# An audio tower with expert-choice routing on one core: experts' rows re-tiled, and the threshold search split anew between VectorE and ScalarE

## The reference

```python
xf = x.reshape(bs, H)                      # 11872 x 128, layer-normed
Sm = jax.nn.softmax(xf @ W_router + b_router, axis=-1)      # 32 experts
G_ek, idx_ek = jax.lax.top_k(Sm.T, k)      # k = 11872 // 32 = 371 tokens for each expert
tokens = xf[idx_ek]
up = einsum(tokens of the group's 4 experts, W_up) + b_up   # 128 -> 341
Eout = silu(up) @ W_down + b_down                           # 341 -> 128
y = zeros.at[idx_ek].add(G_ek * Eout)      # scatter-add, and then h + y
```

## Time and profile before

| | us |
|---|---|
| median of 3 runs | 1569.08 |
| lowest, highest | 1546.99, 1583.76 |
| the profiled execution | 1576.75 |
| its span | 1575.0 |
| phase one | 0 to 1023.4 |
| threshold search | 1023.4 to 1128.6 |
| expert phase | 1128.6 to 1575.0 |

### The profile page before, as it was taken

One profiled execution on the slowest core, in us unless ns is written; L12 is line 12 of the kernel. 1 busy time (PEld: TensorE's weight loads), 2 busy tenths in 40 slices (PEclk: granted clock), 3 DMA queues, 4 the chain that ended last, 5 costly groups with the idle time before them and its releaser, 6 DMA issues.

```text
span 1575.0 us, 23738 instructions
## 1 busy us (share of the span) xinstructions
PE 1123.0 (71%) x7213; PEld 907.3 (58%) x7213; DVE 956.8 (61%) x2599; ACT 447.3 (28%) x968; POOL 604.4 (38%) x406
## 2 busy tenths in 40 slices
PE   5789879888878879879879888500267566667762
PEld 4667667677766767667657667400155455545551
DVE  2566797787787777796787777588723223232220
ACT  2132342342343232341332431433222112121210
POOL 4131221221221221221231230100168888878885
PEclk8677889879879778888788876655568667776766
DMA  2000100101001000100100100000134333333322
GB/s 71 1 16 7 33 27 19 33 28 35 14 30 32 13 26 18 32 27 13 35 26 15 35 10 17 29 12 0 29 59 69 53 62 69 54 61 59 67 42 22
DMA packets 113765, 51.13 MB, mean 32 GB/s; under 512 B 55360, under 2 KB 109920, under 8 KB 113696
## 3 DMA queue, kind: packets, MB, share of 16 engines
q1 hardware_dynamic: 49696, 36.23, 7.9%
q0 software_dynamic: 64000, 14.18, 7.2%
HBM read 30.14 MB, written 19.76 MB: 32 GB/s over the span
## 4 chain that ended last, share of the span: by engine, by line
PE 41%; issue 22%; DVE 16%; POOL 12%; DMA 6%; ACT 2%; DVEq 1%; POOLq 0%; SPq 0%; ACTq 0%
PE pa L773 6%; POOL out_dram L582 6%; PE ps L828 6%; PE pa L798 4%; POOL qd L572 4%; PE po L867 4%; PE pc L889 3%; DVE eqk L1121 3%; DMA out_dram<-tqk,idx 3%; DMA qd<-token_rows,idx 3%; PE pa L775 2%; PE pst L844 2%; PE pa L814 2%; PE po L857 1%; PE pst L842 1%
## 5 line engine op out<-in xcount | busy, mean ns | idle before, releaser
L518 POOL TENSOR_TENSOR rs<-ve,expo 106x7 f32<-106x7 f32 x48 | 71.1, 1482 | 598.2 <-DVE ve L1029 598.2
L582 POOL DMA_INDIRECT out_dram<-tqk,idx x96 | 219.2, 2283 | 46.6 <-issue 30.2
L572 POOL DMA_INDIRECT qd<-token_rows,idx x96 | 131.2, 1367 | 95.5 <-issue 86.4
L773 PE MATMUL pa<-wc,xT 128*106 128x128 f32 x896 | 135.3, 299 | 6.2 <-DMA wc<-in_L_tok_kernel_dram 6.2
L955 PE MATMUL po<-qb 114*124 114x128 f32 (+1 forms) x576 | 133.8, 400 | 1.8 <-ACT qb L730 1.8
L828 PE MATMUL ps<-qb,kd 128*106 128x212 f32 x448 | 132.7, 427 | 0.8 <-ACT kt L681 0.8
L773 PEld LDWEIGHTS pa<-wc,xT 128*106 128x106 f32 x896 | 116.9, 188 | 19.4 <-issue 8.5
L939 PE MATMUL pa<-ident,qd 124*128 124x124 f32 (+1 forms) x96 | 26.4, 408 | 134.3 <-DMA qd<-token_rows,idx 134.3
L955 PEld LDWEIGHTS po<-qb 114*124 114x124 f32 (+1 forms) x576 | 118.7, 298 | 2.8 <-issue 1.4
L529 POOL TENSOR_TENSOR qb<-qd,head_scale 64x1484 f32<-64x1484 f32 x32 | 91.9, 2873 | 67.9 <-DVE qd L1114 46.5
L867 PEld LDWEIGHTS po<-vm,P 106*53 106x53 f32 x1792 | 116.7, 141 | 0.5
(11 more groups left out here) (229 smaller groups left out, 2543.7 us busy)
## 6 DMA issues: line engine op xcount, KB each, us to landing
token_rows<-row SPq DMA_DIRECT2D x16, 463.8 KB
xT<-in_x_cols_dram SPq DMA_DIRECT2D x17, 374.5 KB, 4.4
out_dram<-h SPq DMA_DIRECT2D x16, 371.0 KB
kd<-in_L_ffn_W_up_dram SPq DMA_DIRECT2D x32, 170.5 KB
xr<-in_x_rows_dram SPq DMA_DIRECT2D x17, 224.0 KB, 10.3
qb<-in_L_ffn_W_down_dram SPq DMA_DIRECT2D x32, 114.0 KB
qb<-in_L_ffn_W_down_dram SPq DMA_DIRECT2D x32, 56.5 KB
qd<-token_rows,idx POOLq DMA_INDIRECT x96
```

The costliest lines, as they stand in the source:

```text
L518: eng.tensor_tensor(rs[:, :], ve[:, :], expo[0:C, 0, :], ALU.pow).then_inc(S[root_done], 1)
L572: eng.indirect_dma_start(out=xg[0:n, e.par, t, :], out_offset=None, in_=rows[:, :], in_offset=bass.IndirectOffsetOnAxis(ap=idx[0:n, e.k, t ...
L582: eng.indirect_dma_start(out=out_rows, out_offset=bass.IndirectOffsetOnAxis(ap=idx[0:n, e.k, t:t + 1], axis=0), in_=yw[0:n, e.par, t, :], ...
L773: eng.matmul(dst, xT[:, b.par, a:a + C], wc[:, t, :], start=(t == 0), stop=False)
```

## The change

Three things are changed together.

The experts' 371 rows lie in tiles that start at slots 0, 128 and 254. The scatters take 128, 126 and 117 rows of them. The gathers take 128, 128 and 117 rows: the second one fetches two rows that also stand at the start of the third tile, and they are not used. The slot numbers run to 382 instead of 372, and a few of their results are not used either.

In every round of the search VectorE counts 1,424 keys instead of 2,000, and ScalarE 1,544 instead of 968. ScalarE's unused output goes to the space of `tqk` instead of `xT`, which is too small for it.

The count between the two searches is done like one more round: VectorE counts 1,424 keys, ScalarE 1,544, and the goal of the second search is corrected for ScalarE's way to count.

```diff
--- before.py
+++ after.py
@@ -26,9 +26,11 @@
     F = w_up.shape[2]
     CAP = N // NE
     FC = 114
-    SL = 124
+    SL = 128
+    SLOT0, GOT, PUT = (0, 128, 254), (128, 128, 117), (128, 126, 117)
+    SLOTS = SLOT0[2] + SL
     ROW = D + NE
-    DVE_KEYS = 2000
+    DVE_KEYS = 1424
     SEG = 128 // NE
     JS = NJ // SEG
     ACT_HALF = SEG * (JS * C - DVE_KEYS) / 2
@@ -37,7 +39,7 @@
     QH = LO // 2
     LAM = 1.0 / (1.0 + 1e-07)
     EPS_W, EPS_LN, EPS_DEN = 1e-07, 1e-05, 1e-05
-    assert GS == 4 and 2 * HC == C and NC * C == LO and HALO >= C + TAPS - 1 and CAP * NE == N and 3 * FC == F + 1
+    assert GS == 4 and 2 * HC == C and NC * C == LO and HALO >= C + TAPS - 1 and CAP * NE == N and 3 * FC == F + 1 and sum(PUT) == CAP
 
     ctx = ExitStack()
     with ctx:
@@ -141,7 +143,7 @@
 
         seg_probs = qb[:, 0].rearrange("p k a b -> p (k a b)")
         seg_hits = qb[:, 1, 0].rearrange("p a b -> p (a b)").bitcast(bf16)
-        signs = xT[:, 1, :].bitcast(bf16)[:, 0:JS * C - DVE_KEYS]
+        signs = tqk[:, :, :].rearrange("p a b -> p (a b)").bitcast(bf16)[:, 0:JS * C - DVE_KEYS]
         halves = seg_probs.bitcast(u16).rearrange("p (n two) -> p n two", two=2)
         high = qb[:, 1, 1].rearrange("p a b -> p (a b)").bitcast(u16)
         low = kd[:, 0].rearrange("p a b -> p (a b)").bitcast(u16)
@@ -150,7 +152,7 @@
         same_expert = sb("same_expert", [128, 128], f16)
         bit = sb("bit", [128, 2])
         cand = sb("cand", [128, 1])
-        hits = sb("hits", [128, 2], f16)
+        hits = sb("hits", [128, 1], f16)
         sign_sum = sb("sign_sum", [128, 1], f16)
         half_expert = sb("half_expert", [128, 128], f16)
         target = sb("target", [128, 2])
@@ -164,15 +166,15 @@
         above = sb("above", [C, C], bf16)
         upto = sb("upto", [C, C], bf16)
         before = sb("before", [NJ, NJ], bf16)
-        slots_h = sb("slots_h", [NJ, CAP + 1], f16)
-        slots_f = sb("slots_f", [C, CAP + 1])
+        slots_h = sb("slots_h", [NJ, SLOTS], f16)
+        slots_f = sb("slots_f", [C, SLOTS])
         mask = sb("mask", [C, 1 + 2 * NJ], bf16)
         cnt = sb("cnt", [NJ, 2], bf16)
         cex = sb("cex", [NJ, 2])
 
-        reach = hnT[0:NJ, :].bitcast(bf16)[:, 0:2 * (CAP + 1)].rearrange("p (h n) -> p h n", h=2)
+        reach = hnT[0:NJ, :].bitcast(bf16)[:, 0:2 * SLOTS].rearrange("p (h n) -> p h n", h=2)
         dcum = sb("dcum", [NJ, 2, C], bf16)
-        inside = sb("inside", [C, CAP + 1], bf16)
+        inside = sb("inside", [C, SLOTS], bf16)
         wrap = sb("wrap", [SL, 3])
         idx = sb("idx", [SL, 4, 3], i32)
 
@@ -504,9 +506,9 @@
                                        pattern=[[1, C]], channel_multiplier=-1))
                 step(eng.affine_select(out=before[:, :], in_=before[:, :], compare_op=ALU.is_gt, fill=0.0, base=0,
                                        pattern=[[1, NJ]], channel_multiplier=-1))
-                step(eng.iota(slots_h[:, :], pattern=[[1, CAP + 1]], base=0, channel_multiplier=0,
+                step(eng.iota(slots_h[:, :], pattern=[[1, SLOTS]], base=0, channel_multiplier=0,
                               allow_small_or_imprecise_dtypes=True))
-                step(eng.iota(slots_f[:, :], pattern=[[1, CAP + 1]], base=0, channel_multiplier=0,
+                step(eng.iota(slots_f[:, :], pattern=[[1, SLOTS]], base=0, channel_multiplier=0,
                               allow_small_or_imprecise_dtypes=True))
                 assert made[0] == N_CONSTS
 
@@ -559,16 +561,13 @@
                 eng.wait_ge(row_out[p], 16 * NB // 2)
             out_rows = out.rearrange("b t d -> (b t) d")
 
-            def rows_of(t):
-                return SL if t < 2 else CAP - 2 * SL
-
             def part2(stage, what, e):
                 if (stage, what) == ("I", "idx"):
                     hold(eng, "idx_done", e.count(1, 1))
                     hold(eng, "xgt_ps", e.count(1, 1, back=2))
                     hold(eng, "gcol_done", e.count(2, 2, back=2))
                     for t in range(3):
-                        n = rows_of(t)
+                        n = GOT[t]
                         eng.indirect_dma_start(
                             out=xg[0:n, e.par, t, :], out_offset=None, in_=rows[:, :],
                             in_offset=bass.IndirectOffsetOnAxis(ap=idx[0:n, e.k, t:t + 1], axis=0)
@@ -578,7 +577,7 @@
 
                     hold(eng, y_out, e.count(48, 0))
                     for t in range(3):
-                        n = rows_of(t)
+                        n = PUT[t]
                         eng.indirect_dma_start(
                             out=out_rows, out_offset=bass.IndirectOffsetOnAxis(ap=idx[0:n, e.k, t:t + 1], axis=0),
                             in_=yw[0:n, e.par, t, :], in_offset=None, compute_op=ALU.add).then_inc(y_out, 16)
@@ -712,8 +711,11 @@
 
             eng.wait_ge(S["keys_done"], 2)
             count_signs(high, HIGH_BITS, 0, 0)
+            hold(eng, "thr_step", 2)
+            eng.activation(signs, high[:, DVE_KEYS:], ACT.Sign, scale=-1.0, bias=thr_high[:, 1:2],
+                           accum_out=sign_sum[:, :]).then_inc(S["signs_done"], 1)
             eng.wait_ge(S["keys_done"], 3)
-            count_signs(low_tied, LOW_BITS, 2 + 3 * HIGH_BITS, HIGH_BITS)
+            count_signs(low_tied, LOW_BITS, 2 + 3 * HIGH_BITS, HIGH_BITS + 1)
             eng.wait_ge(S["bup_in"], 16 * 3 * NG)
             eng.wait_ge(S["ones_done"], 1)
 
@@ -908,25 +910,19 @@
             run(eng, part)
             turn(GROUPS - 1)
 
-            def sum_hits(value, signs_value):
-
-
+            def sum_hits(value):
                 need(eng, "hits_done", value)
                 eng.matmul(pst[:, 0:1], same_expert[:, :], hits[:, 0:1], start=True, stop=False)
-                if signs_value is None:
-                    mm = eng.matmul(pst[:, 0:1], same_expert[:, :], hits[:, 1:2], start=False, stop=True)
-                else:
-                    need(eng, "signs_done", signs_value)
-                    mm = eng.matmul(pst[:, 0:1], half_expert[:, :], sign_sum[:, :], start=False, stop=True)
-                mm.then_inc(S["hits_ps"], 1)
+                need(eng, "signs_done", value)
+                eng.matmul(pst[:, 0:1], half_expert[:, :], sign_sum[:, :], start=False, stop=True).then_inc(S["hits_ps"], 1)
 
             with eng.Fori(0, HIGH_BITS // 2) as r:
                 for k in range(2):
-                    sum_hits(r * 2 + (k + 1), r * 2 + (k + 1))
-            sum_hits(HIGH_BITS + 2, None)
+                    sum_hits(r * 2 + (k + 1))
+            sum_hits(HIGH_BITS + 1)
             with eng.Fori(0, LOW_BITS // 2) as r:
                 for k in range(2):
-                    sum_hits(r * 2 + (HIGH_BITS + 2 + k + 1), r * 2 + (HIGH_BITS + k + 1))
+                    sum_hits(r * 2 + (HIGH_BITS + 1 + k + 1))
             eng.wait_ge(S["thr_step"], 8)
             eng.transpose(pst[0:C, 0:NE], thr_wide[:, :], ident[0:NE, 0:NE]).then_inc(S["thr_ps"], 1)
 
@@ -935,8 +931,8 @@
                     need(eng, x_got[e.par], e.half() * 48)
                     need(eng, "xgt_sb", e.count(1, 1, back=1))
                     for t in range(3):
-                        n = SL if t < 2 else CAP - 2 * SL
-                        mm = eng.transpose(p_xg[:, t * SL:t * SL + n], xg[0:n, e.par, t, 0:D], ident[0:n, 0:n])
+                        n = PUT[t]
+                        mm = eng.transpose(p_xg[:, SLOT0[t]:SLOT0[t] + n], xg[0:n, e.par, t, 0:D], ident[0:n, 0:n])
                     mm.then_inc(S["xgt_ps"], 1)
                 if stage == "F" and what in UP:
                     need(eng, w_in[e.k], e.m * 64 + 64)
@@ -950,9 +946,9 @@
                     need(eng, "yw_done", e.count(2, 2, back=1))
                     need(eng, "act_done", e.count(3, 3))
                     for t in [DOWN.index(what)]:
-                        n = SL if t < 2 else CAP - 2 * SL
+                        n = GOT[t]
                         for k in range(3):
-                            mm = eng.matmul(p_dn[0:n, t * D:(t + 1) * D], act[:, e.par, k, t * SL:t * SL + n],
+                            mm = eng.matmul(p_dn[0:n, t * D:(t + 1) * D], act[:, e.par, k, SLOT0[t]:SLOT0[t] + n],
                                             wdn[:, e.k, k, :], start=(k == 0), stop=(k == 2))
                     if what == DOWN[-1]:
                         mm.then_inc(S["dn_ps"], 1)
@@ -985,12 +981,12 @@
                     need(eng, "dcum_sb", e.count(1, 1))
                     need(eng, "inside_done", e.count(1, 1, back=1))
                     for h in range(2):
-                        mm = eng.matmul(p_cum[0:C, 0:CAP + 1], dcum[:, h, :], reach[:, h, :], start=(h == 0), stop=(h == 1))
+                        mm = eng.matmul(p_cum[0:C, 0:SLOTS], dcum[:, h, :], reach[:, h, :], start=(h == 0), stop=(h == 1))
                     mm.then_inc(S["cum_ps"], 1)
                 if (stage, what) == ("I", "idx"):
                     need(eng, "inside_done", e.count(1, 1))
```

(15 more changed lines are left out.)

## The result

The changed kernel takes 1453.36 us (median of 4 runs, 1439.7 to 1465.69) against 1565.26 us before (median of 4, 1546.99 to 1583.76): ratio 0.929, 95% interval 0.916 to 0.943. I had forecast 1475 with a range from 1455 to 1550: the direction and the mechanism held, the gain of 112 us was larger than the 94 of the sum, and the median lies 1.6 us outside the range. Some executions are slower at times, rarely at a far lower granted clock (one of run e9 took 1641 us at 0.53, its others 1444 to 1447), and every ratio here is of the faster runs of both kernels. The profiled execution took 1465.69 us, the longest of the four.

The account below looks back on a forecast made before the run. The bound differed by stage: VectorE in the search, GpSimd's issue time in the middle expert phase. Gains of 17.4 + 1.7 + 62.4 + 9.3 + 3.0 = 93.8 us gave 1483, less the profile's 7.7 offset 1475 us, range 1455 to 1550.

Parts of the forecast that it names:

- Search rounds and count: Search: 30 rounds at 0.58 us less give 17.4 us; the count between the searches saves 1.7 us.
- How the rows are spread: Scatter transfers: rows split equally over as many engines as divide them; each third tile's landing gains 1.6 us.
- What GpSimd pays: Expert phase: issue cost follows rows per engine, falling to 1.12 us a gather and 1.78 a scatter; chance 0.50.
- The floor: Expert phase: GpSimd's issue time plus gaps for one expert, forecast at 10.5 us.
- The period: Middle of the expert phase: time per expert falls from 13.10 to 10.95 us, 62.4 us over 29 experts.
- The loop over two iterations: Expert phase: gathers, landing, TensorE and VectorE, gap and scatters close over two iterations, 20.3 to 21.9 us together.
- The ends: Expert phase: cheaper scatters and landings save 9.3 us at the end; gathers and a landing 3.0 at the start.
- level issue: Rival, expert phase: GpSimd's issue time does not depend on the spread; 1536 us, chance 0.27.
- blocks: Rival, expert phase: GpSimd writes each engine's list in blocks of up to 16 rows; slower, 1710 us, chance 0.12.
- the tiles change nothing: Rival, expert phase: the spread has another cause than divisors, so only the search gains; 1550 us, chance 0.08.
- The signs: What the later profile should show, including GpSimd's share in the middle falling from 84% to some 80%.

Follow-up runs that it names:

- e9: Repeat of e5's order (gathered-row transposes behind the second down tile) on the changed kernel, on one chip with a repeat of the changed kernel: 1446.76 us, ratio 0.925.
- e4: Changed kernel with scatters of 128, 116 and 127 rows and gathers of 128, 128 and 127: 1712.29 us, one run.
- e5: Changed kernel with the transposes of the gathered rows moved from ahead of the first down tile to behind the second: 1430.87 us, ratio 0.915.
- e3: Changed kernel with scatters of 128, 122 and 121 rows and gathers of 128, 128 and 121: 1489.42 us, one run.
- e1: The new tiles only, with the old search (2,000 and 968 keys) and the old count between the searches: 1468.89 us.
- e6: Changed kernel with the gathered-row transposes behind all down projections and the output step, and prefix matmuls ahead of the up projections: 1453.33 us, ratio 0.940.

## Why the prediction was off

Two steps failed in their size, both on the side of a greater gain: what a row on an engine costs GpSimd to issue, and the period of the expert phase.

- **Search rounds and count**: 17.4 + 1.7 = 19.1 us forecast, 20.2 measured. Right, both engines level; the rounds gave 18.5 us, a little above my 15 to 18. In the count between the searches VectorE goes from 3.37 to 1.63 us until `low_tied` starts.
- **How the rows are spread**: right. A third tile lands 1.6 us sooner behind its issue (3.5 to 1.9), the value I took. The Trainium skill ("DMA: Bandwidth & Descriptors", section on why a DMA increments its semaphore by 16) gives the number of engines as the largest number up to 16 that divides the slowest dimension of both sides. The packets of nine tile sizes here agree with it for indirect DMAs. Its exception, 16 engines for some direct copies from GpSimd, is seen in none of these indirect ones.
- **What GpSimd pays: the first step that failed.** I took the slope from tiles 31 and 41 rows deep, 9.5 and 19.5 ns a row. Compared tile by tile at the same position, it is 13.5 to 14.9 ns for a gather and 25.7 to 27.3 for a scatter from there down to 8 or 9 rows (for example from 2.229 to 1.637 us over 23 rows for the first scatter, means of 32). From 9 rows up to 127 in e4 it is 13.3 and 26.5. The two points lay 10 rows apart, and the difference between them was 0.04 and 0.07 us short of what the later slope makes of 10 rows. Most of that is position, since I compared a third tile with the mean of the first two. At 9 rows the third scatter takes 1.584 us and the second 1.607, and the first, 1.637 at 8 rows, would take 1.66 (an estimate by the slope): the third is 0.05 us cheaper than their mean. For gathers it is 0.03. Where the last 0.01 or 0.02 us come from stays open. The floor came out at 9.65 us instead of 10.53.
- **The period: the second.** 10.95 forecast, 10.30 measured, 81.2 us in 29 experts instead of 62.4. The loop over two iterations was named and does bind now (e5 shows it), but at 20.6 us. One turn in the middle is 3.6 for the gathers (issued from 1391.18 to 1394.80), 3.5 for their landing (1398.34), 6.7 to `yw` (1405.04), 1.0 until the scatter starts (1406.05) and 5.8 for the scatters, with gaps. I had 4.0, 3.1 to 4.7, 6.7, 0.3 and 6.2. Of the 1.3 us between my upper end of 21.9 and 20.6 the cheaper issues are 0.8, and the start behind `yw`, 0.7 too short, goes the other way. The rest is the landing: I took its upper end of 4.7, although 3.1 was my own value for a shorter landing, and 3.5 came.
- **The ends**: 9.3 and 3.0 us forecast, 8.2 and 2.4 measured. Close.
- **The whole**: the period was 18.8 us too small and the search 1.1, the ends were 1.7 too large, and phase one took 1.1 more: 111.1 us of gain in the profiles instead of 93.8. The other 4.6 us of the miss have no mechanism: the profiled execution lay 12.3 us above the median, and I had taken 7.7 over from the kernel before. Without them the median would lie inside the range, though the two steps above would be as wrong as they are.
- **Rivals**: level issue is refuted by the timeline. So are blocks, which asked for a first scatter of 3.78 us where 1.64 was measured, and e3 refutes them again (61 rows on each of 2 engines would have been as cheap as 8 blocks). That the tiles change nothing is refuted by e1. The Trainium skill (same page, on where the fixed 2 us goes) says that many descriptors can be emitted before their cost shows. No run here agrees: from 8 steps of rows to 127 every step cost about 14 ns in a gather and 26 in a scatter.
- **The signs**: GpSimd's share in the middle fell to 76% (227.5 of 298.6 us), not to 80%.
- **The range**: its lower end allowed only for my floor of 10.5 us and 7 us of scatter. The bounds of the slope, from two points, should have been wider on the side of the gain; I had bounded it only towards no gain.

## What to carry to other kernels

When GpSimd issues indirect DMAs back to back, choose tile sizes by rows divided by their largest divisor up to 16, for issue and for landing: 126 and 117 rows are cheap, 122, 124 and 127 are not. A few rows fetched twice to reach 128 cost little: a second gather of 128 rows was issued in 0.98 us, a third one of 117 in 0.99. When such a bound engine gets a fifth faster, look for the loop through landings that closes next, and put work that does not need the landing ahead of the work that does, but try it, since a later place can close another loop (e6). Do not extend a slope from two points that lie close together without a bound on both sides.

## What the runs showed of the hardware

- An indirect scatter-add of n rows made 16 x n / k + 16 packets, k the largest divisor of n up to 16. This holds exactly for n = 116, 117, 123, 124 and 126 to 128, each by itself, and for 121 and 122 together. Issue took about 0.87 + 0.014 x n / k us for a gather of 640-byte rows and 1.4 + 0.026 x n / k for a scatter-add of 512-byte rows, within 0.1 us in all of them.
- Three issues of one kind in a row differ by position at equal n / k: of two gathers of 128 rows the first took 1.04 us and the second 0.98, and at n / k = 9 the second scatter took 1.61 and the third 1.58.
- With n / k = 127 (127 rows) the landing of a scatter-add came 8.4 us behind its issue; with 9 (117 rows), 1.9 us.
- Where a scatter group had waited for the landing of the one ahead, GpSimd's first DMA started 0.8 to 0.97 us behind it, in every trace.
- In a wait of 5.25 us TensorE's granted clock fell from 1.00 to 0.50, and a down tile took 1.61 us instead of 0.90.
